# A hyperbolic attention score whose last reciprocal moves from two ScalarE activations to one GpSimd power

## The chip, the core and the metric

The kernel runs on one core of a Trainium2 chip. The core has five engines with queues of their own: TensorE (PE in the rows, its weight loads PEld), VectorE (DVE), ScalarE (ACT), GpSimd (POOL) and SyncE (SP, which here only issues DMAs). They run side by side and meet only at semaphores. The metric is the device time of one execution in microseconds (us), lower is better.

## The reference, cut to what matters

The program is a stack of four small layers, each an attention-like part and a feed-forward part, over 2 sequences of 2048 tokens and 128 channels. The change is in the attention of the third layer. It has 16 heads of 8 channels, 6 with a dot product, 4 with a hyperbolic distance and 6 with a cosine. For the 4 hyperbolic heads the reference does

```python
tq = sqrt(1.0 / curv + sum(q * q, axis=-1, keepdims=True))
tk = sqrt(1.0 / curv + sum(k * k, axis=-1, keepdims=True))
inner = einsum('bhtd,bhsd->bhts', q, k) - tq * swapaxes(tk, -1, -2)
arg = maximum(-curv * inner, 1.0 + 1e-07)
dis = sqrt(1.0 / curv) * arccosh(arg)
scores = 1.0 / (eps + dis) + causal_bias
out = einsum('bhts,bhsd->bhtd', softmax(scores, axis=-1), v)
```

The line that matters is `scores = 1.0 / (eps + dis)`: one reciprocal for each pair of a query and a key that it may see.

## The kernel before

**Tiles.** `hyperbolic` calls `causal_pass` with the name `hypb`. Two heads and both sequences are done in one turn of a hardware loop, so there are two turns (`pairs` is 2). Inside a turn the causal scores are cut into 40 steps, one for each chunk of 512 queries (`qc`) and tile of 128 keys (`st`) that it sees. Each step is done for sequence 0 and for sequence 1, which gives `nh` = 80 items a turn and 160 in all. An item is a tile of 128 keys by up to 512 queries for two heads, that is 128 partitions by 1024 columns; next to the diagonal only 384, 256 or 128 of the 512 queries are left. So 112 items have 1024 columns, and 16 each have 768, 512 and 256.

**The chain of one item n.** PE writes the argument of arccosh into PSUM. Then the item passes between DVE and ACT, in one buffer `u` of a ring of four:

1. DVE `clip`: `a` = max(argument, least) (L1725) and `u` = a*a (L1727)
2. ACT `root`: log of u-1 (L1789) and exp of half of it (L1790), which is sqrt(a*a-1)
3. DVE `plus`: u = a + u (L1732)
4. ACT `cosh`: log (L1796), which is arccosh
5. DVE `scale`: u = u*root(1/curv) + 1e-6, one instruction for each of the two heads (L1740), then the semaphore `scaled`
6. ACT `score`: log (L1803) and exp of minus it (L1804), which is the reciprocal, then `logged`
7. DVE `shift`: minus the row's greatest score, from the tile `mb` (L1747)
8. ACT `exps`: exp into `P` (L1810)
9. DVE `hide`: on diagonal items only, the mask (L1756)
10. PE `weigh`: P times the values (L1368), and DVE `collect` copies the sums out once a chunk (L1410)

**Order.** The order on each engine is written out by hand, two items at a time ("a pair" below). In its steady state DVE does shift(n), plus(n+2), hide(n), scale(n+2), clip(n+4), each for both items of the pair. ACT does root(n+2), exps(n), cosh(n+2), score(n+2). PE runs ahead by up to three items. POOL copies the values of the turn into `hypb_vq` (L1339) at a turn's start and has nothing else to do. A turn starts with loads and with eight copies into `mb` (L1717).

Of the kernel before, what the change touches and what calls it, by code (L numbers as in the profile page):

```python
# [15 lines left out]
ALU = mybir.AluOpType  # L16
ACT = mybir.ActivationFunctionType
# [4 lines left out]
CH = 512  # L22
# [85 lines left out]
def wait(eng, sem, value, alone=None):  # L108


    eng.wait_ge(sem, value)
    if alone is not None:
        eng.sem_inc(alone, 1)
# [1175 lines left out]
STEPS = [(qc, st, 128 * max(st - 4 * qc, 0)) for qc in range(CPB) for st in range(4 * qc + 4)]  # L1289


def causal_pass(nc, name, loads, rows, pairs, head0, values, o_dram, z_dram, mask_b, ident_b, chain=None):
# [4 lines left out]
    nh = 2 * len(STEPS)  # L1297
    SP_RING, P_RING = 3, 4
    with Scope(nc, name) as sc:
# [8 lines left out]
        alone, sp_waits = sc.sem("pool_waits"), sc.sem("sp_waits")  # L1308
        n_dma = [0]
        ch = chain(sc, P, s_ps) if chain else None  # L1310
        with nc.Block() as block:
            @block.sync
            def _(sp):
                with sp.Fori(0, pairs) as hp:

                    sp.wait_ge(summed, (hp + 1) * nh)
                    n_dma[0] = 0
                    for j in range(4):
                        at = slice(64 * (j % 2), 64 * (j % 2) + rows)
                        n_dma[0] += loads(sp, q[at, j // 2, :], k[at, j // 2, :], hp * 2 + j % 2, j // 2, loaded)  # L1320
                    if ch:
                        n_dma[0] += ch["load"](sp, hp, loaded)
                    wait(sp, o_copied, hp * CPB + (CPB + 1), sp_waits)
                    for j in range(4):
                        head = hp * 2 + (j % 2 + head0)
                        tok = slice((j // 2) * S, (j // 2 + 1) * S)
                        sp.dma_start(o_dram[bass.ds(head * HD, HD), tok], o_sb[32 * j:32 * j + HD, :]).then_inc(o_stored, 16)
                        sp.dma_start(z_dram[bass.ds(head * HD, HD), tok], o_sb[32 * j + HD:32 * j + 2 * HD, :]).then_inc(o_stored, 16)
                    wait(sp, o_stored, (hp + 1) * 128, sp_waits)

            @block.gpsimd
            def _(pool):
                pool.memset(vq[:, :, :, :], 1.0).then_inc(pool_step, 1)
                pool.wait_ge(pool_step, 1)
                with pool.Fori(0, pairs) as hp:
                    wait(pool, summed, (hp + 1) * nh, alone)
                    for b in range(B):
                        src = values[:, b * ST:(b + 1) * ST, bass.ds(hp * 2 * HD + head0 * HD, 2 * HD)]
                        pool.tensor_copy(vq[:, :, 2 * b:2 * b + 2, 0:HD], src.rearrange("p t (v d) -> p t v d", v=2)).then_inc(v_ready, 1)  # L1339

            @block.tensor
            def _(pe):
# [317 lines left out]
def hyperbolic(nc, C, W, loads, m, m_hyp, values, o_dram, z_dram, io, ident_b, masks):  # L1660
# [5 lines left out]
    with Scope(nc, "hyp") as sc:  # L1666
# [16 lines left out]
        def chain(sc2, P, s_ps):  # L1683
            mr = sc2.sb("mr", [3, 4, S], BF16)
            mb = sc2.sb("mb", [128, CPB, 4, CH])
            a, u = sc2.sb("a", [128, 4, 2, CH]), sc2.sb("u", [128, 4, 2, CH])
            roots = sc2.sb("roots", [128, 2])
            freed, spread, m_done = sc2.sem("freed"), sc2.sem("spread"), sc2.sem("m_done")
            clipped, rooted, added, logged, shifted = (sc2.sem(n) for n in ("clipped", "rooted", "added", "logged", "shifted"))
            cosh_done, scaled = sc2.sem("arccosh"), sc2.sem("scaled")  # L1690
# [88 lines left out]
            def act_part(act, pairs, nh, scored, exped, summed):  # L1779
                act.sem_inc(exped, RING)  # L1780
                act.sem_inc(freed, RING)
                act.sem_inc(exp_raw, 4)
                act.preload_act_table_set("natural_log_exp_and_others")

                def root(hp, n):
                    lo = STEPS[n // 2][2]
                    at = u[:, n % 4, :, lo:]
                    act.wait_ge(clipped, hp * nh + (n + 1))
                    steps(act.activation(at, at, ACT.Ln, bias=C["minus_one"]))  # L1789
                    act.activation(at, at, ACT.Exp, scale=0.5).then_inc(rooted, 1)  # L1790

                def cosh(hp, n):
                    lo = STEPS[n // 2][2]
                    at = u[:, n % 4, :, lo:]
                    act.wait_ge(added, hp * nh + (n + 1))
                    act.activation(at, at, ACT.Ln).then_inc(cosh_done, 1)  # L1796

                def score(hp, n):

                    lo = STEPS[n // 2][2]  # L1800
                    at = u[:, n % 4, :, lo:]
                    act.wait_ge(scaled, hp * nh + (n + 1))
                    steps(act.activation(at, at, ACT.Ln))  # L1803
                    act.activation(at, at, ACT.Exp, scale=-1.0).then_inc(logged, 1)  # L1804

                def exps(hp, n):
                    lo = STEPS[n // 2][2]
                    act.wait_ge(shifted, hp * nh + (n + 1))
                    act.wait_ge(summed, hp * nh + (n + 1 - 4 + nh))
                    act.activation(P[:, n % 4, :, lo:], u[:, n % 4, :, lo:], ACT.Exp).then_inc(exp_raw, 1)  # L1810

                steps = Steps(act, own_a)
                with steps.loop(pairs, 2 * nh + 1) as hp:

                    steps(act.activation(roots[:, :], W["hyp_root"][:, bass.ds(hp * 2, 2)], ACT.Copy))
                    for f in (root, cosh, score):
                        f(hp, 0)
                        f(hp, 1)
                    for n in range(0, nh, 2):
                        for f, at in ((root, n + 2), (exps, n), (cosh, n + 2), (score, n + 2)):  # L1820
                            if at < nh:
                                f(hp, at)
                                f(hp, at + 1)

            return dict(load=load_m, pe=pe_part, dve=dve_part, act=act_part, freed=freed)

        causal_pass(nc, "hypb", loads, rows, N_HYP // 2, N_DOT, values, o_dram, z_dram, masks["big_kq"], ident_b, chain)


# [914 lines left out]
```

## Time and the profile before

| What | Value |
| --- | --- |
| median of 3 runs | 6929.41 us (6923.68 to 6935.76) |
| the profiled execution's own time | 6921.02 us |
| span of its trace, first to last instruction | 6919.2 us |
| the stretch of `hypb` in it | about 2810 to 3740 us from the span's start |
| ScalarE busy over the whole span | 60% |
| VectorE busy over the whole span | 75% |
| GpSimd busy over the whole span | 26% |

The profile is of one execution. Its own time stands beside its span, since what a stage costs is read inside the span, and the whole is compared by the time. The shares over the whole span are averages of stages with different limits; only the stretch of `hypb` bears on the change.

### The profile page before, as it was taken

The page shows a single profiled execution, that of the slowest core. Times are in us where ns is not written, and L with a number is a line of the kernel's source. Part 1 is how long each engine was busy: PE and PEld are TensorE (multiplying, and loading weights), DVE is VectorE, ACT ScalarE, POOL GpSimd, SP SyncE. Part 2 cuts the span into 40 slices and gives each one's busy share as a digit, 9 for nine tenths or more (in the row PEclk, how much of TensorE's full clock was granted, in tenths as well). Part 3 has the DMA queues.
Part 4 walks back from the last instruction along what each step waited for, and adds up shares of the span by engine and source line. Part 5 has one row for each costly group of instructions (what it writes and reads, how often), then busy time and mean ns, then how long its engine had stood idle before and what let it go on. Part 6 is the DMA issues. An engine that isn't in the chain of part 4 may idle for free. (4 is left out here: it accounts for less than half of the span.)

```text
span 6919.2 us, 84441 instructions
## 1 busy us (share of the span) xinstructions
PE 5147.8 (74%) x23563; PEld 1831.3 (26%) x23563; DVE 5178.2 (75%) x6483; ACT 4138.5 (60%) x5955; POOL 1827.9 (26%) x1241
## 2 busy tenths in 40 slices
PE   4499987879548778332333688888867999999999
PEld 2133332333212222000000122222214444444443
DVE  5399996343667664697896699999974888888887
ACT  3466664424445446798896699999971333333333
POOL 0077773000010000000000000000001777777776
PEclk7699998879779889555555799999996999999999
DMA  0000000000032130000001233332331101111110
GB/s 18 26 1 0 0 0 18 15 0 0 17 107 40 21 64 14 15 0 14 0 0 37 58 44 39 44 40 40 45 37 34 27 20 31 31 25 23 31 31 13
DMA packets 205415, 176.97 MB, mean 26 GB/s; under 512 B 145523, under 2 KB 186751, under 8 KB 196831
## 3 DMA queue, kind: packets, MB, share of 16 engines
q1 hardware_dynamic: 205038, 172.33, 13.0%
q8 instruction: 190, 3.11, 0.2%
q14 instruction: 187, 1.52, 0.1%
HBM read 121.05 MB, written 51.23 MB: 25 GB/s over the span
## 5 line engine op out<-in xcount | busy, mean ns | idle before, releaser
L2076 DVE TENSOR_REDUCE cs_neg<-cs_s_ps 128x1 f32<-128x1024 f32 x1024 | 1185.0, 1215 | 67.1 <-PE cs_s_ps L1940 49.1
L1994 ACT ACTIVATE cs_E<-cs_s_ps,cs_neg 128x1024 f32<-128x1024 f32 x1024 | 1136.6, 1115 | 69.1 <-DVE cs_neg L2076 61.5
L2349 ACT ACTIVATE da_P<-da_P 128x1024 f32<-128x1024 f32 x512 | 541.2, 1057 | 931.4 <-DVE da_P L2424 912.4
L2390 POOL TENSOR_TENSOR da_psum<-da_psum,da_P 128x1024 f32<-128x1024 f32 x384 | 904.9, 2356 | 367.2 <-ACT da_P L2349 334.3
L2407 DVE TENSOR_REDUCE da_mx<-da_s_ps 128x1 f32<-128x1024 f32 x512 | 623.8, 1220 | 199.3 <-PE da_s_ps L2273 199.2
L1368 PE MATMUL hypb_o_ps<-hypb_P,hypb_vq 128*32 128x512 f32 (+3 forms) x640 | 193.6, 932 | 608.6 <-DVEq L1758 404.6
L2424 DVE TENSOR_TENSOR da_P<-da_s_ps,da_lift 128x1024 f32<-128x1024 f32 x512 | 600.6, 1215 | 3.5 <-PE da_s_ps L2277 3.4
L1940 PE MATMUL cs_s_ps<-cs_q,cs_k 64*128 64x512 bf16 x2048 | 401.9, 396 | 261.4 <-ACT cs_E L1994 220.5
L2273 PE MATMUL da_s_ps<-da_k,da_q 64*128 64x512 f32 x2048 | 552.3, 617 | 22.3 <-DMA da_v<-vf 16.2
L1951 PE MATMUL cs_r_ps<-cs_E,cs_w 128*32 128x512 f32 x4096 | 550.8, 612 | 2.5 <-POOL cs_w L2036 0.9
L568 POOL TENSOR_TENSOR scan_hC<-scan_h,scan_c_sb 128x512 f32<-128x512 f32 x256 | 400.2, 1583 | 559.7 <-DVE scan_h L605 558.3
L2287 PE MATMUL da_o_ps<-da_P,da_v 128*64 128x512 f32 x2048 | 495.9, 605 | 0.0
L2277 PE MATMUL da_s_ps<-da_q,da_k 64*128 64x512 f32 x2048 | 482.8, 590 | 0.0
L1570 DVE TENSOR_REDUCE cos_mu<-cos_m_ps 128x1 f32<-128x512 f32 (+1 forms) x480 | 262.2, 604 | 129.2 <-PE cos_m_ps L1529 86.1
L1558 ACT ACTIVATE cos_P<-cos_s_ps 128x1024 f32<-128x1024 f32 (+1 forms) x240 | 203.7, 893 | 205.3 <-PE cos_s_ps L1507 118.1
L482 PE MATMUL scan_y_ps<-scan_hC,consts 128*128 128x512 f32 x512 | 286.5, 645 | 37.8 <-POOL scan_hC L568 17.9
L1558 ACT ACTIVATE dot_P<-dot_s_ps 128x1024 f32<-128x1024 f32 (+1 forms) x240 | 201.9, 894 | 176.0 <-PE dot_s_ps L1507 118.4
L605 DVE TENSOR_TENSOR_SCAN scan_h<-scan_dA,scan_carry,scan_dBx 128x512 f32<-128x512 f32 x192 | 302.9, 1617 | 0.1
L2028 POOL TENSOR_TENSOR cs_gap<-cs_low,cs_neg 128x16 f32<-128x16 f32 x64 | 13.9, 217 | 1006.7 <-DVE cs_low L2082 1006.7
L1940 PEld LDWEIGHTS cs_s_ps<-cs_q,cs_k 64*128 64x128 bf16 x2048 | 98.4, 93 | 635.2 <-ACT cs_E L1994 561.7
L2277 PEld LDWEIGHTS da_s_ps<-da_q,da_k 64*128 64x128 f32 x2048 | 197.8, 187 | 240.0 <-issue 224.1
L1570 DVE TENSOR_REDUCE dot_mu<-dot_m_ps 128x1 f32<-128x512 f32 (+2 forms) x320 | 174.7, 604 | 90.5 <-PE dot_m_ps L1529 55.2
(448 smaller groups left out, 9294.1 us busy)
## 6 DMA issues: line engine op xcount, KB each, us to landing
da_q<-qf SPq DMA_DIRECT2D x32, 512.0 KB, 8.8
da_k<-kf SPq DMA_DIRECT2D x32, 512.0 KB, 10.5
cs_q<-q_parts SPq DMA_DIRECT2D x384, 32.0 KB
cs_k<-k_parts SPq DMA_DIRECT2D x384, 32.0 KB
qf<-cs_side_sb SPq DMA_DIRECT2D x32, 256.0 KB, 3.5
kf<-cs_side_sb SPq DMA_DIRECT2D x32, 256.0 KB, 5.3
vf<-cs_side_sb SPq DMA_DIRECT2D x32, 256.0 KB, 5.7
da_v<-vf SPq DMA_DIRECT2D x16, 512.0 KB, 11.6
```

Of the source, the lines that this page charges most:

```text
L1570: dve.tensor_reduce(mu[:, x % 2, i, o // CH:o // CH + 1], m_ps[:, u % M_RING, 0:w], AX.X, ext["op"]).then_inc(reduced, 1)
L1940: mm = pe.matmul(s_ps[:, seg.slot(u, RING, 2), c * CH:(c + 1) * CH], k[half, p, i * 128:(i + 1) * 128], q[half, p, at], start=True, stop=True)
L1951: mm = pe.matmul(r_ps[32 * a:32 * a + 32, :], weight, E[:, seg.slot(t, E_RING), a // 2, (a % 2) * CH:(a % 2 + 1) * CH], start=(i == 0), st ...
L1994: act.activation(E[:, seg.slot(t, E_RING), h, :], s_ps[:, seg.slot(u, RING, 2), :], ACT.Exp, bias=neg[:, g, j, h:h + 1], accum_out=z[:, g, ...
L2076: dve.tensor_reduce(neg[:, g, j, h:h + 1], s_ps[:, seg.slot(u, RING, 2), :], AX.X, ALU.max, negate=True).then_inc(maxed, 1)
L2273: mm = pe.matmul(s_ps[:, slot, c, :], q[half(c), p, tile * 128:(tile + 1) * 128], k[half(c), p, part * CH:(part + 1) * CH], start=True, st ...
L2277: mm = pe.matmul(s_ps[:, slot, c, :], k[half(c), p, kt * 128:(kt + 1) * 128], q[half(c), p, (quad % CPB) * CH:(quad % CPB + 1) * CH], star ...
L2287: mm = pe.matmul(o_ps[half(c), :], v[:, p, 2 * u + c, :], P[:, g % RING, c, :], start=(u == 0), stop=(u == UNITS - 1))
L2349: act.activation(P[:, g % RING, :, :], P[:, g % RING, :, :], ACT.Exp).then_inc(exped, 1)
L2390: pool.tensor_tensor(psum[:, :, :], psum[:, :, :], P[:, g % RING, :, :], ALU.add).then_inc(pooled, 1)
L2407: dve.tensor_reduce(mx[:, g // UNITS % 2, g % UNITS // 2, g % 2:g % 2 + 1], s_ps[:, slot, :, :].rearrange("p c n -> p (c n)"), AX.X, ALU.m ...
L2424: dve.tensor_tensor(P[:, g % RING, :, :], s_ps[:, slot, :, :], lift[:, quad % 2, :].unsqueeze(1).to_broadcast([128, 2, CH]), ALU.add).then ...
```

## The change

`score` leaves ACT. In its place POOL gets one instruction for each item: it waits for `scaled`, raises `u` in place to the power of a second operand, a column of -1 that is repeated over the item's columns, and signals `logged`. DVE's code isn't touched; it waits for the same semaphore.

```diff
+                    if ch:
+                        ch["pool"](pool, hp, nh, alone)
...
-                def score(hp, n):
-
-                    lo = STEPS[n // 2][2]
-                    at = u[:, n % 4, :, lo:]
-                    act.wait_ge(scaled, hp * nh + (n + 1))
-                    steps(act.activation(at, at, ACT.Ln))
-                    act.activation(at, at, ACT.Exp, scale=-1.0).then_inc(logged, 1)
...
-                    for f in (root, cosh, score):
+                    for f in (root, cosh):
                         f(hp, 0)
                         f(hp, 1)
                     for n in range(0, nh, 2):
-                        for f, at in ((root, n + 2), (exps, n), (cosh, n + 2), (score, n + 2)):
+                        for f, at in ((root, n + 2), (exps, n), (cosh, n + 2)):
...
+            def pool_part(pool, hp, nh, alone):
+                for n in range(nh):
+                    at = u[:, n % 4, :, STEPS[n // 2][2]:]
+                    wait(pool, scaled, hp * nh + (n + 1), alone)
+                    power = C["minus_one"].unsqueeze(2).to_broadcast([128, 2, CH - STEPS[n // 2][2]])
+                    pool.tensor_tensor(at, at, power, ALU.pow).then_inc(logged, 1)
```

On ACT, in the steady state of a turn, one pair of whole items reads like this before (the REGISTER_ALU rows prepare a wait; `x2` means two items):

```order
1001 L1789 ACTIVATE hypb_u<-hypb_u,consts 128x1024
1002 L111 REGISTER_ALU
1003 L1790 ACTIVATE hypb_u<-hypb_u 128x1024
1004 L1788 REGISTER_ALU
1005 L1789 ACTIVATE hypb_u<-hypb_u,consts 128x1024
1006 L111 REGISTER_ALU
1007 L1790 ACTIVATE hypb_u<-hypb_u 128x1024
1009 L1810 ACTIVATE hypb_P<-hypb_u 128x1024
1011 L1810 ACTIVATE hypb_P<-hypb_u 128x1024
1012 L1796 ACTIVATE hypb_u<-hypb_u 128x1024 x2
1013 L1803 ACTIVATE hypb_u<-hypb_u 128x1024
1015 L1804 ACTIVATE hypb_u<-hypb_u 128x1024
```

And in the changed kernel, where L1791 and L1792 are the two of `root`, L1804 is `exps` and L1798 is `cosh`:

```order
971 L1791 ACTIVATE hypb_u<-hypb_u,consts 128x1024
972 L111 REGISTER_ALU
973 L1792 ACTIVATE hypb_u<-hypb_u 128x1024
975 L1791 ACTIVATE hypb_u<-hypb_u,consts 128x1024
976 L111 REGISTER_ALU
977 L1792 ACTIVATE hypb_u<-hypb_u 128x1024
979 L1804 ACTIVATE hypb_P<-hypb_u 128x1024
981 L1804 ACTIVATE hypb_P<-hypb_u 128x1024
982 L1798 ACTIVATE hypb_u<-hypb_u 128x1024 x2
```

Twelve activations a pair have become eight, and the rest keep their order. On POOL a turn of the loop was this before:

```order
198 L1335 ISA
199 L1339 ISA
200 L1339 COPY hypb_vq<-l_values 128x16x2x8
201 L1339 ISA
202 L1339 COPY hypb_vq<-l_values 128x16x2x8
203 L1335 REGISTER_ALU
204 L1335 COMPARE_AND_BRANCH
```

In the changed kernel 80 powers, each with its wait, stand behind those two copies; the first are these:

```order
202 L1339 COPY hypb_vq<-l_values 128x16x2x8
203 L111 ISA
204 L1824 TENSOR_TENSOR hypb_u<-hypb_u,consts 128x1024
205 L111 REGISTER_ALU
206 L1824 TENSOR_TENSOR hypb_u<-hypb_u,consts 128x1024
207 L111 REGISTER_ALU
208 L1824 TENSOR_TENSOR hypb_u<-hypb_u,consts 128x2x384
```

The two copies of a turn are ahead of the powers, so no copy is moved behind one; the next turn's copies stand behind the 80th power.

## Rows read from the trace of the kernel before

**Rows 1.** The page: busy tenths in 40 slices of 173 us each

```profile
DVE  5399996343667664697896699999974888888887
ACT  3466664424445446798896699999971333333333
POOL 0077773000010000000000000000001777777776
```

**Rows 2.** The two turns' windows: length; busy PE, PEld, DVE, ACT, POOL

```profile
2820.50:3264.50 444.00, 138.55 (x540) 25.32 (x538) 397.26 (x516) 423.56 (x480) 0.71 (x2) 0.56 0.00 0
3296.00:3739.70 443.70, 138.85 (x540) 25.39 (x538) 397.12 (x516) 423.60 (x480) 0.00 (x0) 0.56 0.00 0
```

**Rows 3.** Waits in 2821 to 3740: waiter, released by, total, times, longest

```profile
ACT hypb_u L1789 <- DVE hypb_u L1727: 73.4, 16, 33.6
DVE hypb_u L1740 <- ACT hypb_u L1796: 50.9, 58, 1.1
```

**Rows 4.** Timeline, one steady pair: start, us, engine, line

```profile
3149.24 1.22 DVE L1725 TENSOR_SCALAR hypb_a<-hypb_s_ps 128x1024 f32<-128x1024 f32 x1
...
3154.03 2.35 DVE L1747 TENSOR_TENSOR hypb_u<-hypb_u,hypb_mb 128x1024 f32<-128x1024 f32 x2
...
3159.72 1.83 DVE L1740 TENSOR_SCALAR hypb_u<-hypb_u,hypb_roots 128x512 f32<-128x512 f32 x4 [1.06 <-ACT hypb_u L1796]
3160.64 1.06 ACT L1803 ACTIVATE hypb_u<-hypb_u 128x1024 f32<-128x1024 f32 x1
...
3161.46 1.22 DVE L1725 TENSOR_SCALAR hypb_a<-hypb_s_ps 128x1024 f32<-128x1024 f32 x1
```

**Rows 5.** Groups by line and shape on ACT, 2780 to 3760

```profile
L1804 ACT ACTIVATE hypb_u<-hypb_u 128x1024 f32<-128x1024 f32 x112 | 118.3, 1057 | 3.6
L1803 ACT ACTIVATE hypb_u<-hypb_u 128x1024 f32<-128x1024 f32 x112 | 117.4, 1048 | 1.6 <-DVE hypb_u L1740 1.5
```

**Rows 6.** Groups by line and shape on DVE, 2780 to 3760

```profile
L1732 DVE TENSOR_TENSOR hypb_u<-hypb_a,hypb_u 128x1024 f32<-128x1024 f32 x112 | 132.5, 1219 | 5.3 <-ACT hypb_u L1790 5.3
L1747 DVE TENSOR_TENSOR hypb_u<-hypb_u,hypb_mb 128x1024 f32<-128x1024 f32 x112 | 131.8, 1218 | 0.0
L1740 DVE TENSOR_SCALAR hypb_u<-hypb_u,hypb_roots 128x512 f32<-128x512 f32 x224 | 98.2, 483 | 51.5 <-ACT hypb_u L1796 48.4
L1756 DVE TENSOR_TENSOR hypb_P<-hypb_P,l2w_wt 128x256 f32<-128x256 f32 x64 | 25.1, 420 | 3.9 <-ACT hypb_P L1810 3.9
L1732 DVE TENSOR_TENSOR hypb_u<-hypb_a,hypb_u 128x512 f32<-128x512 f32 x16 | 10.3, 685 | 0.0
```

**Rows 7.** Groups by line and shape on POOL, whole span

```profile
L2390 POOL TENSOR_TENSOR da_psum<-da_psum,da_P 128x1024 f32<-128x1024 f32 x384 | 904.9, 2356 | 367.2 <-ACT da_P L2349 334.3 <-POOL da_psum L2390 32.5 <-POOL da_psum L2387 0.3
L568 POOL TENSOR_TENSOR scan_hC<-scan_h,scan_c_sb 128x512 f32<-128x512 f32 x256 | 400.2, 1583 | 559.7 <-DVE scan_h L605 558.3 <-PE scan_y_ps L482 1.4
L2395 POOL TENSOR_TENSOR da_zs<-da_psum 128x512 f32<-128x512 f32 x64 | 82.3, 1286 | 10.7 <-issue 9.2 <-POOL da_psum L2390 1.5
L2021 POOL COPY cs_side_x<-xn 128x128 f32 x30 | 8.7, 289 | 2.9 <-issue 1.6
L1339 POOL COPY hypb_vq<-l_values 128x256 f32 x4 | 1.5, 399 | 465.4 <-PE hypb_o_ps L1368 465.0 <-POOL hypb_vq L1333 0.5
L1333 POOL MEMSET hypb_vq<- 128x2048 f32 x1 | 1.8, 1804 | 219.0 <-POOLq L1243 219.0
L2735 POOL MEMSET const-float32-1.0<- 128x1 f32 x1 | 0.1, 108 | 0.0
```

**Rows 8.** Timeline, start of the second turn's loop and end of the stage

```profile
3295.91 1.22 DVE L1725 TENSOR_SCALAR hypb_a<-hypb_s_ps 128x1024 f32<-128x1024 f32 x1 [1.03 <-PE hypb_s_ps L1357]
...
3305.31 1.04 ACT L1803 ACTIVATE hypb_u<-hypb_u 128x1024 f32<-128x1024 f32 x1
...
3736.43 0.42 ACT L1804 ACTIVATE hypb_u<-hypb_u 128x256 f32<-128x256 f32 x1
...
3739.03 0.69 DVE L1410 COPY hypb_o_sb<-hypb_o_ps 128x512 f32<-128x512 f32 x1 [0.75 <-PE hypb_o_ps L1368]
```

More of the change, by code:

```diff
@@ L1812, in act_part @@
                 steps = Steps(act, own_a)
-                with steps.loop(pairs, 2 * nh + 1) as hp:
+                with steps.loop(pairs, nh + 1) as hp:
                     steps(act.activation(roots[:, :], W["hyp_root"][:, bass.ds(hp * 2, 2)], ACT.Copy))
-                    for f in (root, cosh, score):
+                    for f in (root, cosh):
                         f(hp, 0)
@@ L1823, in act_part @@
                                 f(hp, at + 1)
-            return dict(load=load_m, pe=pe_part, dve=dve_part, act=act_part, freed=freed)
+            def pool_part(pool, hp, nh, alone):
[4 more added lines that the diff above has]
+                    pool.tensor_tensor(at, at, power, ALU.pow).then_inc(logged, 1)
+            return dict(load=load_m, pe=pe_part, dve=dve_part, act=act_part, pool=pool_part, freed=freed)
         causal_pass(nc, "hypb", loads, rows, N_HYP // 2, N_DOT, values, o_dram, z_dram, masks["big_kq"], ident_b, chain)
```

## The prediction

> **What bounds the kernel now.** I read the slices of the page first, to see who works in the stretch of `hypb`, which is about slices 17 to 21 of 40 [rows 1]. The reader sees DVE and ACT at 9 tenths both and POOL at 0. Next the two windows, one for each turn's loop, from the first `clip` to the last `collect`: 444.0 and 443.7 us, together 887.7. ACT is busy for 847.2 of them, DVE for 794.4, PE for 277.4 [rows 2]. So ACT is the fullest engine by 53 us, and DVE is close behind. Then the waits: ACT waits for DVE 16 times, and two of those are the starts of turns, up to 33.6 us long; in the steady state it hardly waits. DVE waits 58 times for `cosh`, 50.9 us in all [rows 3]. One steady pair of whole items in the timeline shows this again: from `clip` to the same `clip` two items on is 12.22 us, and the one gap on DVE is the 1.06 us ahead of `scale` [rows 4]. ACT sets the pace; if it were free, DVE could win back those 50.9 us and little more.
>
> **What the change removes.** On ACT the 160 logs and 160 exps of `score`, 1.05 and 1.06 us each for a whole item [rows 5]. That is 2.1 of ACT's some 6.3 us per item. Alone it would give 51 us, the wait of DVE, since DVE's own work is then the bound: 6921 - 51 = 6870 us.
>
> **What it adds.** On POOL 160 powers, which stand in series between `scale` and `shift`. POOL is empty there, so nothing else is pushed away. Call the price of a power p for a whole item. Two paths hold:
>
> First the slack. The power of item n may start when `scale`(n) ends. DVE still does `scale`(n+1) and two `clip`s of 2.4 us each ahead of `shift`(n), then `shift`(n) itself, so `shift`(n+1) would start some 0.9 + 4.7 + 1.2 = 6.8 us after that point. Both powers fit in while 2p is under 6.8 us, so up to p = 3.4 us they cost nothing. The cover is then DVE's `clip`.
>
> Second, beyond it, the loop. DVE works in order, so `plus`(n+2) and `scale`(n+2) are queued behind `shift`(n+1), which waits for the second power of the pair; and the next power waits for `scale`(n+2). POOL is therefore idle in every pair for `shift`(n+1) 1.22, two `plus` 2.44 and the two instructions of `scale`(n+2) 0.97 [rows 6], about 4.6 us, and with a little for the hand-over 4.7. ACT's `exps` and `cosh` of the same moment lie beside the two `plus`, and the `clip`s lie under the powers. The cycle of a pair is then 2p + 4.7 us, against 12.22 now. It breaks even at p = 3.7 to 3.8 us.
>
> Now the sum over all items. Columns: 112 x 1024 + 16 x (768 + 512 + 256) = 139,264. With c ns for a column and 0.1 us for each instruction (the smallest POOL row takes 108 ns [rows 7]) POOL works 139.3c + 16 us. The idle part is 56 whole pairs x 4.7 = 263; 24 narrow pairs at about 3.7 (for the middle width `plus` takes 0.69 us, and the 0.42 us mask stands there twice [rows 6]) = 89; and the mask in the 8 diagonal pairs of whole width, 6: together 358. Each turn has a start, from `clip` to the first `score`, of 3305.31 - 3295.91 = 9.4 us, and a tail, from the last exp's end at 3736.85 to the end of the copy at 3739.72, of 2.9 [rows 8]: two turns, some 24. The time is
>
> 6921 - 887.7 + 24 + 358 + 16 + 139.3c = 6431 + 139.3c us.
>
> It is the present time at c = 3.5 ns. What lies ahead of the stage, after it and between the turns isn't touched.
>
> **The price of a power.** No row shows it, so I bound it. From below: POOL's two-input TENSOR_TENSOR takes 2356 ns on 1024 columns and 1286 on 512, so 2.09 ns a column [rows 7]; a power reads and writes the same and can't be cheaper, and nothing excludes that it is as cheap. From above there are only steps to count. A power of a free exponent is a log, a product and an exp, which ACT does with tables but other engines must build: split off the exponent, a polynomial of some eight steps, the product, rounding, a second polynomial, put the exponent back, and tests for zero, infinity and negative bases. I count some 40 elementary steps; 25 is lean. What is a step's price? The two-input row does four things in 2.09 ns (two reads, the arithmetic, a write): 0.52 each. The copies do two in (399 - 289)/128 = 0.86 ns: 0.43 each. The memset does one, in (1804 - 108)/2047 = 0.83 ns: 0.83 [rows 7]. The operation is a two-input one, so I take 0.52: c = 40 x 0.52 = 20.9 ns, p = 21.5 us, six times the break-even. The sum is 6431 + 2911 = 9342 us. The median of the runs shown is 8 us above the profiled execution, so I say 9345. DVE working beside POOL could add a little: a multiply on 512 columns takes 1583 ns beside the scan where another two-input row of that size takes 1286 [rows 7]; at up to 0.6 us an item that is under 100 us, and DVE will stand still for most of the time, so I leave it out.
>
> The rows say that software sets POOL's price, and the Trainium skill says so more sharply: its page "GPSIMD Engine Reference", section 3.1, has a loop with three or more operations for an element bound by the slots at roughly three operations a cycle. By that, at the 1.2 GHz that the page uses, 40 steps are an estimated 11.1 ns, and the sum would be 7977 us. Its page "Trainium Architecture — The Big Picture", in "The five engines, in one table", keeps exp and its kind for ScalarE and calls GpSimd the wrong place for streaming elementwise work; no row here has such an operation on POOL.
>
> **The rivals.**
>
> Steps overlap. If three of the steps fit in the beat of 0.83 ns that the memset row shows, 40 steps are 11.1 ns a column, p = 11.5 us, and the time is 6431 + 1546 = 7977 us. For it: a copy does its read and write in the same beat as a memset its write alone. Against it: the two-input row gets four things into two and a half beats. The skill's rule of section 3.1 is this one.
>
> Steps don't overlap, or they branch. At 0.83 ns for each of 40 steps c is 33 ns and the time 6431 + 4597 = 11,028 us. For it: a polynomial is a chain in which each step needs the last. Against it: the same loop has 16 rows of partitions and many columns to interleave, and the copies show overlap.
>
> The power is cheap: the other side. If c is near the add's 2.09, p is 2.4 us, the powers lie under DVE's `clip`, and DVE takes over as the bound: 6870 us, 0.7% faster. This decides below p = 3.4 to 3.7, or 3.5 ns a column, 1.7 times the add. It would need fewer than 7 steps at 0.52 ns, so either a shortcut for an exponent of -1 or a hardware unit. Nothing in the rows speaks for one.
>
> The price just at the break-even, 3.4 to 3.8 us: ACT's relief and POOL's wait cancel, 6921 us. The window is so narrow that I give it little.
>
> **How the numbers follow.** A measurement of this kernel tells about 0.2% from no change. Chances: c of 14 to 30 ns as forecast, 0.50, time 9345; c of 6 to 14, steps overlap, 0.27; c above 30, 0.15; c of 3.6 to 6, a lean power that still costs more than it frees, 0.03; break-even 0.01; cheap and faster 0.04. Slower is 0.95, same 0.01, faster 0.04. The range runs from 25 steps at three to a beat (7 ns, 7400 us) to 40 unoverlapped steps and the add's reads on top (35 ns, 11,300 us); about one in ten lies on either side.
>
> **What would show it.** In the changed profile one group on POOL, 160 instructions, should stand out; its mean on 1024 columns is p, and its means on 768, 512 and 256 columns give c. I expect 21.5 us, POOL at 9 tenths in the stage, and in each pair one idle time of POOL of about 4.7 us ahead of a power, released by `scale`. DVE should wait at `shift` for POOL, for most of the stage, and ACT at `root` or `exps` for DVE; the 50.9 us at `scale` should be gone. The stage should be 2p + 4.7 us a pair, and everything else as before to within 10 us. The prediction would be wrong if p is far from 20 us; the sum then still gives the time from p. It would be wrong in its form if POOL's idle time a pair isn't near 4.7, or if DVE's or ACT's own rows grow beside the powers.

## The result, and the profile after

The changed kernel takes 28,655.96 us in the median of 4 runs (28,648.96 to 28,664.75), the kernel before 6932.59 us. The ratio is 4.134, with a 95% interval of 4.126 to 4.141. Slower was forecast, but by a third, not fourfold: the time lies far outside the range of 7400 to 11,300 us.

The page of the kernel after, in slices of 717 us, answers to [rows 1]:

```profile
span 28663.0 us, 84441 instructions
...
DVE  7755677677775777777557757777577777749787
ACT  5544000000000000000000000000000000039633
POOL 3400999999999999999999999999999999950177
```

POOL is full for some 31 of 40 slices and ACT is empty in them. DVE looks busy too, which no step of the prediction provided for. The groups of the same page say which instructions these are:

```profile
L1824 POOL TENSOR_TENSOR hypb_u<-hypb_u,consts 128x1024 f32<-128x1024 f32 (+3 forms) x160 | 22212.5, 138830 | 452.8 <-DVE hypb_u L1742 452.8
L1742 DVE TENSOR_SCALAR hypb_u<-hypb_u,hypb_roots 128x512 f32<-128x512 f32 (+3 forms) x320 | 10228.3, 32012 | 12.8 <-ACT hypb_u L1798 12.8
L1729 DVE TENSOR_TENSOR hypb_u<-hypb_a 128x1024 f32<-128x1024 f32 (+3 forms) x160 | 5366.0, 33538 | 5.5
L1749 DVE TENSOR_TENSOR hypb_u<-hypb_u,hypb_mb 128x1024 f32<-128x1024 f32 (+3 forms) x160 | 179.9, 1124 | 6474.9 <-POOL hypb_u L1824 6474.9
```

The 160 powers take 22,212.5 us. They alone are more than three times the old kernel. By width, from the groups of POOL that keep shapes apart:

```profile
L1824 POOL TENSOR_TENSOR hypb_u<-hypb_u,consts 128x1024 f32<-128x1024 f32 x112 | 18280.4, 163218 | 363.9 <-DVE hypb_u L1742 363.9
L1824 POOL TENSOR_TENSOR hypb_u<-hypb_u,consts 128x768 f32<-128x768 f32 x16 | 1962.1, 122630 | 39.2 <-DVE hypb_u L1742 39.2
L1824 POOL TENSOR_TENSOR hypb_u<-hypb_u,consts 128x512 f32<-128x512 f32 x16 | 1311.9, 82009 | 28.6 <-DVE hypb_u L1742 28.6
...
L1824 POOL TENSOR_TENSOR hypb_u<-hypb_u,consts 128x256 f32<-128x256 f32 x16 | 658.1, 41143 | 21.1 <-DVE hypb_u L1742 21.1
```

A power of a whole item takes 163.2 us, and the widths give (163.218 - 41.143)/768 = 0.159 us, that is 159 ns, a column. The forecast was 21.5 us and 20.9 ns. The second thing to see is in the DVE rows. Over all widths, one `scale` instruction now takes 32.0 us in the mean and one square of `clip` 33.5. On whole items alone `scale` takes 41.2 us, 0.48 before [rows 6], and the square 36.0 us, 1.23 before. The timeline of one steady pair, which answers to [rows 4], shows where:

```profile
7988.61 163.21 POOL L1824 TENSOR_TENSOR hypb_u<-hypb_u,consts 128x1024 f32<-128x1024 f32 x1 [0.85 <-DVE hypb_u L1742]
7989.60 82.41 DVE L1729 TENSOR_TENSOR hypb_u<-hypb_a 128x1024 f32<-128x1024 f32 x1
8071.93 1.21 DVE L1727 TENSOR_SCALAR hypb_a<-hypb_s_ps 128x1024 f32<-128x1024 f32 x1
...
8151.85 1.23 DVE L1749 TENSOR_TENSOR hypb_u<-hypb_u,hypb_mb 128x1024 f32<-128x1024 f32 x1 [76.32 <-POOL hypb_u L1824]
...
8156.40 163.21 POOL L1824 TENSOR_TENSOR hypb_u<-hypb_u,consts 128x1024 f32<-128x1024 f32 x1 [4.58 <-DVE hypb_u L1742]
8156.48 163.80 DVE L1742 TENSOR_SCALAR hypb_u<-hypb_u,hypb_roots 128x512 f32<-128x512 f32 x2 [0.26 <-ACT hypb_u L1798]
...
8320.46 163.21 POOL L1824 TENSOR_TENSOR hypb_u<-hypb_u,consts 128x1024 f32<-128x1024 f32 x1 [0.85 <-DVE hypb_u L1742]
```

The cycle is 8320.46 - 7988.61 = 331.85 us: two powers, and idle time of POOL, 4.58 us ahead of the first of a pair and 0.85 ahead of the second. `scale` of the second item is issued 0.08 us behind the start of the first power, and its two instructions aren't done until 0.67 us after that power's end, so the second power starts late. A square isn't done until 8072.0, about half way through the second power. Three powers here, beside rows of DVE that stand and rows that don't, take 163.21 us each.

### The profile page after: what moved, and what is told of

Read it like the earlier page. It is cut to its first block and busy times, and to the rows that moved or that the text cites. A ratio compares the mean times of both kernels' runs of the same rounds, so it can differ in the third digit from the quotient of the medians.

```text
span 28663.0 us, 84441 instructions
## 1 busy us (share of the span) xinstructions
PE 5195.3 (18%) x23563; PEld 1833.3 (6%) x23563; DVE 20489.9 (71%) x6483; ACT 3886.6 (14%) x5635; POOL 24040.8 (84%) x1401
## 5 line engine op out<-in xcount | busy, mean ns | idle before, releaser
L1824 POOL TENSOR_TENSOR hypb_u<-hypb_u,consts 128x1024 f32<-128x1024 f32 (+3 forms) x160 | 22212.5, 138830 | 452.8 <-DVE hypb_u L1742 452.8
L1742 DVE TENSOR_SCALAR hypb_u<-hypb_u,hypb_roots 128x512 f32<-128x512 f32 (+3 forms) x320 | 10228.3, 32012 | 12.8 <-ACT hypb_u L1798 12.8
L1729 DVE TENSOR_TENSOR hypb_u<-hypb_a 128x1024 f32<-128x1024 f32 (+3 forms) x160 | 5366.0, 33538 | 5.5
L1749 DVE TENSOR_TENSOR hypb_u<-hypb_u,hypb_mb 128x1024 f32<-128x1024 f32 (+3 forms) x160 | 179.9, 1124 | 6474.9 <-POOL hypb_u L1824 6474.9
L1791 ACT ACTIVATE hypb_u<-hypb_u,consts 128x1024 f32<-128x1024 f32 (+3 forms) x160 | 163.0, 1019 | 15623.6 <-DVE hypb_u L1729 15623.2
L1804 ACT ACTIVATE hypb_P<-hypb_u 128x1024 f32<-128x1024 f32 (+3 forms) x160 | 147.5, 922 | 6436.4 <-DVE hypb_u L1749 6436.4
```

Of the source, the lines that this page charges most:

```text
L1729: dve.tensor_tensor(u[:, n % 4, :, lo:], a[:, n % 4, :, lo:], a[:, n % 4, :, lo:], ALU.mult).then_inc(clipped, 1)
L1742: ins = dve.tensor_scalar(at_v, at_v, roots[:, v:v + 1], 1e-6, ALU.mult, ALU.add)
L1824: pool.tensor_tensor(at, at, power, ALU.pow).then_inc(logged, 1)
```

## The experiments

Two questions were open. Why does a power cost 163 us: its arithmetic, the repeated operand, or DVE beside it? And is the rest of the sum right, the cover and the loop, which the size of the power hides? Of each kernel only the part that the diff shows is changed.

**A price list.** Ahead of the first turn, in the kernel before, POOL does each form once, with a wait between them; `x` holds 3.7, `y` -1 and `u[:, 1]` 0.5.

```diff
+                step(pool.tensor_tensor(z, x, minus, ALU.pow))
+                step(pool.tensor_tensor(z, x, y, ALU.pow))
+                step(pool.tensor_tensor(z, x, one, ALU.pow))
+                step(pool.tensor_tensor(z, x, u[:, 1, :, :], ALU.pow))
+                step(pool.tensor_tensor(z, x, minus, ALU.mult))
+                step(pool.tensor_tensor(flat(z, 128, 512), flat(x, 128, 512), flat(y, 128, 512), ALU.pow))
...
+                step(dve.reciprocal(mb[:, 1, 0:2, :], mb[:, 0, 0:2, :]))
+                step(dve.tensor_tensor(mb[:, 1, 0:2, :], mb[:, 0, 0:2, :], mb[:, 0, 2:4, :], ALU.mult))
```

> The kernel before, with a list of single GpSimd instructions ahead of the first turn of hypb, one at a time, while DVE has three short instructions of its own and then waits. No power is in the loops. Theory A, the power is intrinsically slow arithmetic on a core's 16 rows together: about 163 us on 1024 columns with the repeated -1, with a full tile of -1, with exponent +1 and with 0.5; 82 us on 512 columns, 10 us on 64, 2.6 us on 16, and the same 82 us on 16 partitions and on 1. Theory B, the repeated column (stride 0) is what costs: the full tile is at least three times faster. Theory C, VectorE's instructions beside it stretch it: every form is far under 163 us here. Theory D, it goes element by element inside a core: 1 partition costs a sixteenth of 16. Theory E, the exponent -1 takes a slow path: 0.5 or 1 differ by more than a fifth. The multiply should be 2.4 us or less on all theories. On DVE the reciprocal of 1024 columns has no row so far: if it takes one pass, 1.2 us; if it iterates, some 8 us.

The timeline of this kernel on POOL, in the order of the list (start, us, line):

```profile
2808.29 163.24 POOL L1839 TENSOR_TENSOR hypb_u<-hypb_a,consts 128x1024 f32<-128x1024 f32 x1
2971.61 163.62 POOL L1840 TENSOR_TENSOR hypb_u<-hypb_a 128x1024 f32<-128x1024 f32 x1
3135.31 163.21 POOL L1841 TENSOR_TENSOR hypb_u<-hypb_a,consts 128x1024 f32<-128x1024 f32 x1
3298.60 163.62 POOL L1842 TENSOR_TENSOR hypb_u<-hypb_a,hypb_u 128x1024 f32<-128x1024 f32 x1
3462.30 1.89 POOL L1843 TENSOR_TENSOR hypb_u<-hypb_a,consts 128x1024 f32<-128x1024 f32 x1
3464.27 82.14 POOL L1844 TENSOR_TENSOR hypb_u<-hypb_a 128x512 f32<-128x512 f32 x1
3546.48 10.54 POOL L1845 TENSOR_TENSOR hypb_u<-hypb_a 128x64 f32<-128x64 f32 x1
3557.11 2.90 POOL L1846 TENSOR_TENSOR hypb_u<-hypb_a 128x16 f32<-128x16 f32 x1
3560.08 82.14 POOL L1847 TENSOR_TENSOR hypb_u<-hypb_a 16x512 f32<-16x512 f32 x1
3642.30 82.13 POOL L1848 TENSOR_TENSOR hypb_u<-hypb_a 1x512 f32<-1x512 f32 x1
```

Theory A's numbers came out. The second operand's form (L1839, L1840) and the exponent (-1, 1, 0.5) change the price by 0.4 us at most, and one partition costs as much as 128. Beside the first power DVE had a two-input multiply of its own, beside the third nothing: 163.24 and 163.21 us. The price is some 0.35 us and 159 ns a column; a whole power costs 86 times the multiply in the same list. So B, C, D and E fall. Of D one thing stays open: one filled partition costs as much as 16, but no run shows whether the rows of a core are worked on together or one after the other. DVE's reciprocal took 6.55 us on 1024 columns.

**The change without the power's price.** A multiply stands in the power's place.

```diff
-                    pool.tensor_tensor(at, at, power, ALU.pow).then_inc(logged, 1)
+                    pool.tensor_tensor(at, at, power, ALU.mult).then_inc(logged, 1)
```

> The changed kernel with a multiply by -1 in place of the power, on the same operands and with the same waits, so that its scores are not the reference's. It prices everything about the change but the power itself. By the sum of the prediction (powers under 3.4 us hide under clip, DVE becomes the bound) 6870 us, 0.7% faster than before. The rival: while GpSimd's instruction runs, DVE's scale and its square can't start or finish, as the rows of the changed kernel show; then DVE, which has only 50 us of idle time, loses up to 2 us for each of the 160 items, and the time is 6950 to 7200 us, no faster than before.

It took 7044 us, a ratio of 1.018 (1.015 to 1.020): somewhat slower than before, though ACT is free of a third of its work and POOL is ready long before it is needed. Two groups of DVE tell why:

```profile
L1742 DVE TENSOR_SCALAR hypb_u<-hypb_u,hypb_roots 128x512 f32<-128x512 f32 x224 | 189.7, 891 | 32.8 <-ACT hypb_u L1798 29.7
L1729 DVE TENSOR_TENSOR hypb_u<-hypb_a 128x1024 f32<-128x1024 f32 x112 | 170.5, 1522 | 3.9
```

Against [rows 6] the first has grown by 91.5 us. The second has grown by 33.3 us, as its group in the kernel before shows:

```profile
L1727 DVE TENSOR_TENSOR hypb_u<-hypb_a 128x1024 f32<-128x1024 f32 x112 | 137.2, 1225 | 3.8
```

The rival of the expectation holds, with the price of its lower half.

**Few columns.** The power on 8 and on 32 columns an item:

```diff
-                    at = u[:, n % 4, :, STEPS[n // 2][2]:]
+                    at = u[:, n % 4, :, STEPS[n // 2][2]:STEPS[n // 2][2] + 4]
```

> The changed kernel with the power on only 4 queries of each head, 8 columns an item; the other columns stay without a reciprocal. Price of a power by the changed kernel's slope: 0.1 + 8 x 0.159 = 1.4 us. By the prediction's sum it hides: 6870 us. By the rival in which DVE stands still beside GpSimd: each power takes up to 1.4 us from DVE, 160 x 1.4 = 224 us at most, so 6900 to 7090 us.

> The same with 16 queries of each head, 32 columns an item. Price 0.1 + 32 x 0.159 = 5.2 us, beyond the slack of 3.4 us, in all pairs. The sum of the prediction with p constant over the widths: 6921 - 888 + 24 + 358 + 160 x 5.2 = 7247 us, some 4.6% slower. If DVE's standing still adds the 0.85 us gap that the changed kernel shows ahead of each second power, 80 x 0.85 = 68 us more, 7315 us.

With 8 columns (a power of 1.74 us by its row) the time was 6911 us, ratio 0.998 (0.997 to 0.999). The powers hide, and DVE's rows are those of before: here nothing stands still, so the rival, which needed DVE to lose time, is refuted for such short powers, though its range holds the time. But of the 51 us that were to come back, only 18 did. The group of `scale` still has 32.8 us of idle time ahead of it, 51.5 before [rows 6].

With 32 columns the power took 5.52 us and the time was 7272 us, ratio 1.050 (1.048 to 1.053). With the measured p the sum says 6921 - 888 + 24 + 358 + 160 x 5.52 = 7298 us, 0.4% off. A cover up to some 3.4 us and a cost of 2p for a pair beyond it agree with both kernels; where between 1.74 and 5.52 us the cover ends, no run shows.

**ScalarE's order.** Is the remainder the order on ACT, where `exps` of this pair is queued ahead of `cosh` of the next? On the 8-column kernel:

```diff
-                        for f, at in ((root, n + 2), (exps, n), (cosh, n + 2)):
+                        for f, at in ((root, n + 2), (cosh, n + 2), (exps, n)):
...
+                    pair(scale, n + 2)
                     pair(hide, n)
-                    pair(scale, n + 2)
```

> The kernel with the power on 8 columns an item, but ScalarE does cosh of the next pair ahead of exps, and VectorE does scale ahead of hide. The 8-column kernel took 6911 us and not 6870, with 33 us of VectorE idle ahead of scale. If that remainder is ScalarE's order (exps queued ahead of cosh), the idle goes and the time is 6911 - 33 = 6878 us. If it is something else, no change.

The forecast was missed, in an instructive way: 7115 us, ratio 1.027 (1.025 to 1.029). The timeline of this kernel:

```profile
3204.53 1.99 ACT L1804 ACTIVATE hypb_P<-hypb_u 128x1024 f32<-128x1024 f32 x2
...
3205.68 2.87 PE L1370 MATMUL hypb_o_ps<-hypb_P,hypb_vq 128*32 128x512 f32 x8 [11.39 <-DVEq L1760]
...
3208.48 1.04 PE L1355 MATMUL hypb_s_ps<-hypb_q,hypb_k 54*128 54x512 bf16 x4
3209.13 1.22 DVE L1727 TENSOR_SCALAR hypb_a<-hypb_s_ps 128x1024 f32<-128x1024 f32 x1 [3.59 <-PE hypb_s_ps L1355]
```

The 0.60 us ahead of `scale` in each pair did go; the idle time of its group fell from 32.8 to 14.8 us. But `exps` now ends later, PE's `weigh` waits for it, and PE's next scores are queued behind `weigh`. DVE waits 3.6 us for them at this `clip`, 163.6 us ahead of the `clip`s of whole items in all. So 18 us of what was left are ACT's order, and they can't be had this way: the order that costs them is what keeps PE ahead. The other 14.8 us are not the order. They are some 0.25 us in a pair, in which `scale` of the second item waits for its own `cosh`; a group of 12.8 us with this releaser stands in the changed kernel too, where ACT is almost empty.

**Halves.** The power in two instructions, one for each head, at most 512 columns each; then the multiply likewise.

```diff
-                    pool.tensor_tensor(at, at, power, ALU.pow).then_inc(logged, 1)
+                    for v in range(2):
+                        ins = pool.tensor_tensor(at[:, v, :], at[:, v, :], power[:, v, :], ALU.pow)
+                    ins.then_inc(logged, 1)
```

> The changed kernel with each power cut into two instructions, one for each head, of at most 512 columns. By the prices measured alone (82.1 us on 512 columns against 163.2 on 1024) GpSimd works some 160 x 1.1 = 170 us longer. Theory P, a GpSimd instruction takes in at most 512 columns at a time and holds the interface that VectorE needs only while columns are still to be taken in: now no VectorE row is stretched (scale back from 32 us in the mean to 0.5, the square from 33.5 to 1.2), the 0.85 us gap ahead of each second power goes, and the time is 28656 + 170 - 80 x 0.85 = some 28,760 us. Theory Q, it is held for the whole instruction: scale and square stay as long in sum, and the time is some 28,820 us.

> The kernel with a multiply in place of the power, each cut in two of at most 512 columns; scores are not the reference's. Unsplit it took 7044 us with VectorE's scale at 0.89 and square at 1.52 us. Theory P (held only while columns are still to be taken in): a multiply streams, so it takes its columns in over most of its time, whatever their number: little changes, 7000 to 7060 us. A rival: below 513 columns nothing is ever held: scale and square return to 0.48 and 1.22 us and the time to that of the 8-column kernel, 6911 us.

The halved power took 28,677 us in its one run. DVE's two stretched groups are nearly what they were before the change, and `shift` has grown a little:

```profile
L1742 DVE TENSOR_SCALAR hypb_u<-hypb_u,hypb_roots 128x512 f32<-128x512 f32 x224 | 140.8, 672 | 12.8 <-ACT hypb_u L1798 12.8
L1729 DVE TENSOR_TENSOR hypb_u<-hypb_a 128x1024 f32<-128x1024 f32 x112 | 137.2, 1225 | 3.9
L1749 DVE TENSOR_TENSOR hypb_u<-hypb_u,hypb_mb 128x1024 f32<-128x1024 f32 x112 | 183.7, 1640 | 17873.9 <-POOL hypb_u L1825 17873.9
```

Thousands of busy microseconds are gone from DVE and the time has hardly moved. The halved powers took 22,291 us, 79 more than whole ones, not the 170 that was expected, and the time rose by 21. So some 58 us came back, near the 68 of 80 gaps of 0.85 us: the stretched rows cost the changed kernel these gaps and nothing else that shows. Q is refuted. P isn't whole either, as the timeline shows:

```profile
8151.15 245.69 POOL L1825 TENSOR_TENSOR hypb_u<-hypb_u,consts 128x512 f32<-128x512 f32 x3 [4.58 <-DVE hypb_u L1742]
8151.22 1.64 DVE L1742 TENSOR_SCALAR hypb_u<-hypb_u,hypb_roots 128x512 f32<-128x512 f32 x2 [0.25 <-ACT hypb_u L1798]
...
8314.98 2.05 DVE L1749 TENSOR_TENSOR hypb_u<-hypb_u,hypb_mb 128x1024 f32<-128x1024 f32 x1 [157.33 <-POOL hypb_u L1825]
```

Two `scale` instructions that come 0.07 us behind the start of a power on 512 columns take 1.64 us, 0.88 elsewhere, and a `shift` that comes just behind another one's start takes 2.05, 1.22 elsewhere. So such a power too holds DVE up, for some 0.8 us at its start. The halved multiply took 6989 us, ratio 1.008 (1.006 to 1.010), with `scale` at 0.69 and the square at 1.44 us: below 7044 but far from 6911. So multiplies on at most 512 columns do hold DVE up, for less time; both sides of that expectation missed, and P came nearer.

**DVE beside a power.** A list as above, in which one DVE instruction on 512 columns is issued behind one or three reciprocals, with a power of 512, 640 or 1024 columns under way.

> The kernel before, with a list ahead of the first turn in which one VectorE instruction on 512 columns of SBUF is issued some 7 or 21 us after the start of a GpSimd power, once as the scale form (one input) and once with two inputs. Theory P: beside a power on 512 columns neither waits, early or late: 0.48 and 0.7 us. Beside 640 and 1024 columns both wait: the two-input form until the power has taken in its last columns (for 1024 some half of its 163 us, for 640 some 82 us too), the scale form until its end. Theory Q, held for the whole instruction: all wait to the end at every width. The reciprocals ahead of them, one input at 6.55 us, should never wait.

The timeline, for 512, 640 and 1024 columns: each time the power, and the DVE instruction beside it. The last one was issued 20 us after its power's start, the others 6.5 to 6.6 us.

```profile
2809.14 82.15 POOL L1837 TENSOR_TENSOR hypb_u<-hypb_a 128x512 f32<-128x512 f32 x1 [1.19 <-DVEq L1871]
2815.66 0.49 DVE L1873 TENSOR_SCALAR hypb_mb<-hypb_mb,consts 128x512 f32<-128x512 f32 x1
...
2898.34 0.69 DVE L1878 TENSOR_TENSOR hypb_mb<-hypb_mb 128x512 f32<-128x512 f32 x1
...
3139.52 102.57 POOL L1849 TENSOR_TENSOR hypb_u<-hypb_a 128x640 f32<-128x640 f32 x1 [0.45 <-DVEq L1895]
...
3146.12 96.25 DVE L1897 TENSOR_SCALAR hypb_mb<-hypb_mb,consts 128x512 f32<-128x512 f32 x1
...
3242.70 102.56 POOL L1852 TENSOR_TENSOR hypb_u<-hypb_a 128x640 f32<-128x640 f32 x1 [0.61 <-DVEq L1900]
...
3249.30 75.88 DVE L1902 TENSOR_TENSOR hypb_mb<-hypb_mb 128x512 f32<-128x512 f32 x1
...
3345.71 163.62 POOL L1855 TENSOR_TENSOR hypb_u<-hypb_a 128x1024 f32<-128x1024 f32 x1 [0.45 <-DVEq L1905]
...
3352.31 157.30 DVE L1907 TENSOR_SCALAR hypb_mb<-hypb_mb,consts 128x512 f32<-128x512 f32 x1
...
3509.93 163.61 POOL L1858 TENSOR_TENSOR hypb_u<-hypb_a 128x1024 f32<-128x1024 f32 x1 [0.61 <-DVEq L1910]
...
3516.53 76.68 DVE L1912 TENSOR_TENSOR hypb_mb<-hypb_mb 128x512 f32<-128x512 f32 x1
...
3674.00 163.62 POOL L1861 TENSOR_TENSOR hypb_u<-hypb_a 128x1024 f32<-128x1024 f32 x1 [0.45 <-DVEq L1915]
...
3694.12 63.16 DVE L1919 TENSOR_TENSOR hypb_mb<-hypb_mb 128x512 f32<-128x512 f32 x1
```

Theory P's numbers came out. Beside 512 columns neither form waits (6.5 and 6.6 us after the start here; at 20 us they took 0.49 and 0.69 us too). Beside 640 and 1024 the two-input form is done 82.5 and 83.3 us after the power's start, which is about the price of the first 512 columns; beside 1024 that is so whether it was issued at 6.6 or at 20 us. The scale form is done 0.28 us after the power's end (at 3242.37 and 3509.61). The reciprocal never waited. That POOL takes columns in by blocks of 512, and holds this form up only while it takes them in, is the reading that fits. It would also explain the some 0.8 us of wait at a power's start in the kernel above, and that 83.3 is 0.8 us more than 82.5: the second block has 384 columns more, an estimated 0.8 us at 2.09 ns a column [rows 7]. No row shows POOL's inside.

**The reciprocal on VectorE.** No power; DVE does it behind `scale`.

```diff
                     ins.then_inc(scaled, 1)
+                    dve.wait_ge(scaled, hp * nh + (n + 1))
+                    dve.reciprocal(u[:, n % 4, :, lo:], u[:, n % 4, :, lo:]).then_inc(logged, 1)
```

> The changed kernel with the reciprocal of each item on VectorE, right behind its scale, in place of the power on GpSimd. Measured beside a power, VectorE's reciprocal took 6.55 us on 1024 columns, 6.4 ns a column. VectorE's work in the loops grows from 794 us by 139,264 x 6.4 ns = 891 and becomes the bound: loops of some 794 + 891 + 16 + 70 (starts, the wait ahead of scale, hand-overs) = 1770 us, time 6921 - 888 + 1770 = some 7800 us, 12% slower than before and a quarter of the changed kernel. If the reciprocal's price grows when it reads what VectorE has just written, or holds others up, it is over 7900 us.

It took 7757 us, ratio 1.121 (1.119 to 1.123), 0.6% under the 7800 expected. Its group:

```profile
L1743 DVE RECIPROCAL hypb_u<-hypb_u 128x1024 f32<-128x1024 f32 x112 | 733.9, 6553 | 3.9
```

So one whole reciprocal costs 2.1 us on ACT as log and exp [rows 5], 6.6 us on DVE, and 163 us on POOL. The kernel before has it in the cheapest place; no kernel here that computes the reference is faster than it.

## Why the prediction was wrong

**The price of a power**, the term c of the sum, is the step that failed: "I take 0.52: c = 40 x 0.52 = 20.9 ns, p = 21.5 us". It is 159 ns and 163 us, 7.6 times that. The whole miss is in this one term: 139.3 x (159.4 - 20.9) = 19,290 us of the 19,311 between 9345 and 28,656. Two guesses were multiplied, a count of steps that no row supported and a price of a step taken from rows that move data and hardly compute. At 0.52 ns, 159 ns would be some 306 steps. Which of the two was off, the runs don't tell. The upper end, 35 ns, was the worse fault: it took the same 40 steps and varied only the price of each, so it bounded nothing. "Bound from above" had no row to stand on, and the range should have said so by being open upward. Of the rivals, "Steps don't overlap, or they branch" points the right way, but its 33 ns is a fifth of the price, and the chances gave c above 30 ns only 0.15. "Slower" was forecast rightly and for a right reason, a power above the break-even; the size was not.

**The Trainium skill's rule** of three operations a cycle ("GPSIMD Engine Reference", section 3.1) led further off, to 7977 us with the same count. By its 1.2 GHz 159 ns are 191 cycles a column, an estimate; no trace here shows how many operations they hold. The table in "Trainium Architecture — The Big Picture" ("The five engines, in one table"), which the prediction cites from the Trainium skill too, keeps such work off GpSimd, and here the trace agrees: 163 us for a power on POOL, 2.1 for log and exp on ACT.

**The form of the sum** held up. With the measured powers it gives 6921 - 887.7 + 24 + 358 + 22,212.5 = 28,628 us, 0.1% under the result. POOL's 4.7 us of idle time a pair is 4.58 ahead of the first power; the 0.85 ahead of the second was not foreseen. The kernel with 32 columns fits the same sum within 0.4%. One reading was loose: in slices 17 to 21 of [rows 1] DVE is at 6 to 9 tenths and ACT at 7 to 9, not both at 9; the sum stands on the windows of [rows 2] and isn't touched.

**"DVE's or ACT's own rows grow beside the powers"** was named as a sign of error, and DVE's did. The prediction dismissed this contention as under 100 us. In the changed kernel that is right for the time, since DVE has nothing else to do; the halved power shows it. It is wrong where POOL's instruction is cheap. It also moved the sign that the prediction named: DVE waits at `shift` for POOL for only 6475 us of the stage's some 22,650, because it stands in `scale` and the square for some 15,300 more. In the halved kernel that wait is 21,698 us, as forecast.

**The rival on the other side**, 6870 us with a cheap power, would hardly have come true: with a multiply at 1.9 to 2.0 us the kernel is 1.8% slower. 51 us were to be won. Only 18 of them came back with the power on 8 columns; 18 hang on ACT's order and some 15 on `cosh` of the second item, which the prediction put down to a busy ACT. DVE's stretched rows take some 125 us on whole items, and 7044 is 133 us above 6911. So even at a multiply's price the change would have been slower, by a step that the prediction did not have. The Trainium skill's page "SBUF — State Buffer" ("Who interferes with whom") says of the interface that DVE and GpSimd share that whoever starts first holds it for the whole instruction, and the other waits: a DVE instruction with two SBUF inputs, against a GpSimd one that reads SBUF, or a DVE instruction in a two-port mode. I passed over that rule. In kind the two-input rows fit it, and `scale` would if it runs in such a mode, which no row states. The length doesn't fit for two inputs: beside 1024 columns that form was done at half of the power, and beside 512 it didn't wait 6.5 us after the start. Here the measurement decides.

**Other engines.** ACT's work in the stage fell from 847 to 595 us, and what lies behind the stage stayed as it was: from 25,480 us to the end are 3183 us, against 3179 from 3740 on before.

## What to carry to other kernels

Before work goes to an idle engine, measure that one instruction by itself: one launch settled what counting steps missed by a factor of 7.6. If no row shows an operation, don't build an upper bound from a guessed count; ask instead at what price the change breaks even (here 3.5 ns a column) and how much is known about which side of that it lies. And an idle GpSimd is not free room beside a busy VectorE: even a cheap instruction there can lengthen VectorE's by more than it saves elsewhere.

## What the runs showed of the hardware

- A GpSimd power of float32 costs some 0.35 us and 159 ns a column, for the exponents -1, 1 and 0.5, for a repeated or a full second operand (163.2 and 163.6 us on 1024 columns), and for any number of partitions tried (82.14 us on 128 x 512 and on 16 x 512, 82.13 on 1 x 512).
- Beside a GpSimd power of 640 or 1024 columns, a VectorE multiply with two SBUF inputs was done 82.5 and 83.3 us after the power's start, a scale of one SBUF input 0.28 us after its end, and a reciprocal didn't wait at all. Beside 512 columns none waited 6.5 or 20 us after the start; issued within 0.1 us of the start, scales and a two-input row took some 0.8 us longer.
- Beside 160 GpSimd multiplies of up to 1024 columns (2.0 us each on 1024) a VectorE scale on 512 columns took 0.89 us in the mean, 0.48 without them, and a two-input row on 1024 columns 1.52, 1.23 without them; with the multiplies halved, 0.69 and 1.44.
- VectorE's reciprocal takes 6.55 us on 1024 columns of float32, more than five times the 1.22 of a two-input row of that size.
